# A decoder on one core: two stages rewritten, the maxima and score pieces of the last cross attention and the film sum and bias of the modulation

## The reference, cut to what matters

```python
scores = jnp.einsum('bthd,bghd->bhtg', Q, K) / np.sqrt(DH)
scores = jnp.where(vision_mask[:, None, None, :], scores, -jnp.inf)
topv, topi = jax.lax.top_k(scores, 32)
probs = jax.nn.softmax(topv, axis=-1)
attn = jnp.zeros_like(scores).at[bi, hi, ti, topi].set(probs)
c_t = jnp.einsum('btg,bgd->btd', attn.mean(axis=1), V) * text_mask[..., None]
x = layernorm(x_text, g_norm_in, b_norm_in)
scale_in, shift_in = jnp.split(c_t @ W_film_in + b_film_in, 2, axis=-1)
x = x * (1.0 + mod_gate * scale_in) + mod_gate * shift_in
```

```python
attn = jnp.einsum('bhnd,bhmd->bhnm', q * scale, k)
attn = jax.nn.softmax(attn, axis=-1)
out = jnp.einsum('bhnm,bhmd->bhnd', attn, v)
return out @ proj_w + proj_b
```

## Time and profile before

| | before |
|---|---|
| median of 3 runs | 4454.17 us (4453.13 to 4456.05) |
| the profiled execution's own time | 4449.1 us |
| its span | 4447.3 us |
| granted TensorE clock, mean | 0.819 of full |
| busy: PE, PEld, DVE, ACT, POOL | 76%, 55%, 64%, 41%, 15% |

### The profile page before, as it was taken

One profiled execution on the slowest core, in us unless ns is written; L12 is line 12 of the kernel. 1 busy time (PEld: TensorE's weight loads), 2 busy tenths in 40 slices (PEclk: granted clock), 3 DMA queues, 4 the chain that ended last, 5 costly groups with the idle time before them and its releaser, 6 DMA issues. The chain is left out here.

```text
span 4447.3 us, 71062 instructions
## 1 busy us (share of the span) xinstructions
PE 3383.5 (76%) x21887; PEld 2428.7 (55%) x21951; DVE 2825.5 (64%) x8344; ACT 1819.8 (41%) x5244; POOL 680.4 (15%) x867
## 2 busy tenths in 40 slices
PE   3668379366665885756888867999969997996887
PEld 3546279122223663544556754666657776554777
DVE  6556633599995874365885443444457776566997
ACT  1356234111113663213775333222235554445886
POOL 0044523000003775201000110000000000000000
PEclk9889589566666665577777777999989998998999
DMA  4030167100004000513000000000000000000000
GB/s 115 1 164 0 36 209 234 50 0 0 0 0 154 1 0 18 150 52 90 0 0 0 1 10 0 10 9 9 0 20 0 0 0 3 1 0 15 1 0 19
DMA packets 111454, 152.52 MB, mean 34 GB/s; under 512 B 21594, under 2 KB 88216, under 8 KB 109718
## 3 DMA queue, kind: packets, MB, share of 16 engines
q1 hardware_dynamic: 99822, 142.12, 10.3%
q0 software_dynamic: 11520, 9.05, 0.7%
HBM read 107.45 MB, written 58.50 MB: 37 GB/s over the span
## 5 line engine op out<-in xcount | busy, mean ns | idle before, releaser
L1260 PE MATMUL l_attn_p_s<-l_attn_outer,l_attn_upper 128*128 128x512 f32 x256 | 204.3, 972 | 113.9 <-DVE l_attn_outer L1203 100.0
L95 POOL TENSOR_TENSOR rstd<-vareps,minus_half 128x32 f32<-128x32 f32 x11 | 59.8, 5438 | 1455.7 <-DVE vareps L86 1322.5
L398 ACT ACTIVATE l_ffn_sg<-l_ffn_p_g 112x512 f32<-112x512 f32 x192 | 114.6, 597 | 391.8 <-PE l_ffn_p_g L378 371.9
L409 DVE TENSOR_TENSOR l_ffn_h<-l_ffn_sg,l_ffn_p_u 112x512 f32<-112x512 f32 x192 | 131.8, 687 | 172.6 <-PE l_ffn_p_u L381 172.0
L381 PE MATMUL l_ffn_p_u<-l_ffn_f_xTall,l_ffn_wu 128*112 x384 | 199.1, 600 | 7.3 <-DVE l_ffn_h L409 7.3
L1418 POOL DMA_INDIRECT slots_in<-l_xattn_x,l_xattn_slot x192 | 190.1, 990 | 81.9 <-issue 50.4
L378 PE MATMUL l_ffn_p_g<-l_ffn_f_xTall,l_ffn_wg 128*112 x384 | 199.0, 600 | 0.9 <-DVE l_ffn_al L2450 0.9
L1260 PEld LDWEIGHTS l_attn_p_s<-l_attn_outer,l_attn_upper 128*128 128x128 f32 x256 | 79.2, 324 | 218.6 <-issue 174.2
L387 PEld LDWEIGHTS l_ffn_p_o<-l_ffn_wd,l_ffn_h 112*128 112x128 f32 x1536 | 176.6, 192 | 15.7 <-issue 15.7
L2614 ACT ACTIVATE l_attn_E<-l_attn_p_s,l_attn_nm 128x128 f32<-128x128 f32 x512 | 180.9, 385 | 2.9 <-DVE l_attn_nm L2572 2.9
L387 PE MATMUL l_ffn_p_o<-l_ffn_wd,l_ffn_h 112*128 112x128 f32 x1536 | 176.7, 275 | 0.0
(11 more groups left out here) (790 smaller groups left out, 9505.8 us busy)
## 6 DMA issues: line engine op xcount, KB each, us to landing
l_experts_w<-in_L_ffn_w SPq DMA_DIRECT2D x72, 512.0 KB
slots_in<-l_xattn_empty SPq DMA_DIRECT2D x8, 2145.0 KB, 24.0
shares_out<-l_xattn_zero SPq DMA_DIRECT2D x24, 512.0 KB, 12.5
l_combine_got<-shares_out SPq DMA_DIRECT2D x16, 768.0 KB, 4.5
l_attn_toep<-kernel_rows SPq DMA_DIRECT2D x1, 8192.0 KB, 31.6
xattn_toep<-ssm_rows SPq DMA_DIRECT2D x1, 8192.0 KB
l_slots_w<-in_L_ffn_w SPq DMA_DIRECT2D x32, 176.0 KB
l_experts_x<-slots_in SPq DMA_DIRECT2D x72, 65.0 KB
```

The source lines that it names most:

```text
L398: act.activation(X.sg[:, k % 2], X.p_g[0:X.FP, k % 2], ACT.Silu).then_inc(s.silu_ready, 1)
L409: dve.tensor_tensor(X.h[:, k // X.FC, k % X.FC], X.sg[:, k % 2], X.p_u[0:X.FP, k % 2], ALU.mult).then_inc(s.h_ready, 1)
L1260: mm = pe.matmul(p_s[:, r, a], upper[:], outer[:, r, a * 512:(a + 1) * 512], start=True, stop=True)
```

## The change

In `l3_xattn` the scores of an item are written in one piece, after the whole of the item before has been read; VectorE takes all maxima by one instruction, and ScalarE exponentiates by one. The turned maxima are copied once (`nmT`), without masks; the masks move into a constant, `pick`, which is made once, and 16 matmuls of 128 columns take the place of the 4 of 512.

In `l2_film` VectorE's search is cut: rounds 0 and 1, then the film sum, then rounds 2 and 3. The bias goes to TensorE as three rows of bfloat16 that add up to the float32 row, with a stationary matrix of three rows of ones; the rows are made once by eight instructions at the phase's start, behind the preparation of `wf` and `bf`.

```diff
@@ l2_film, VectorE
+                dve.tensor_copy(ones3[:], R.ones[0:3, :])
...
-                last.then_inc(s.set_ready, 1)
+                chain(last)
+                for r in range(3):
+                    whole = bf[0:3] if r == 0 else brest[:]
+                    chain(dve.tensor_copy(bpart[:], whole))
+                    if r == 0:
+                        chain(dve.tensor_scalar(bparts[:], bpart[:], R.ident[0:3, 0:1], None, ALU.mult))
+                    else:
+                        last = dve.scalar_tensor_tensor(out=bparts[:], in0=bpart[:], scalar=R.ident[0:3, r:r + 1], in1=bparts[:],
+                                                        op0=ALU.mult, op1=ALU.add)
+                        if r == 2:
+                            last.then_inc(s.set_ready, 1)
+                            break
+                        chain(last)
+                    chain(dve.tensor_tensor(brest[:], whole, bpart[:], ALU.subtract))
+                def searched(u, rounds):
+                    for r in rounds:
+                        src = sc[:, u % 2] if r == 0 else wk[:]
+                        for h in range(H):
+                            last = dve.max(top[:, h, 8 * r:8 * r + 8], src[:, h])
+                        if r == TOP // 8 - 1:
+                            last.then_inc(s.top_ready, 1)
+                            break
+                        chain(last)
+                        if r == 0:
+                            dve.tensor_scalar(nm[:], top[:, :, 0], -1.0, None, ALU.mult).then_inc(s.max_ready, 1)
+                        for h in range(H):
+                            last = dve.match_replace(wk[:, h], top[:, h, 8 * r:8 * r + 8], src[:, h], -3e38)
+                        chain(last)
...
-                        for r in range(TOP // 8):
...
+                        searched(u, (0, 1))
                     for b, u in item(3):
                         dve.wait_ge(s.film_done, b + 1)
                         chain(dve.tensor_tensor(f[:], xr[:, u % 2], p_f[:, 0:P], ALU.mult))
                         dve.tensor_tensor(row(xin, b), f[:], p_f[:, P:256], ALU.add).then_inc(s.xin_done, 1)
+                    for b, u in item(1):
+                        searched(u, (2, 3))
@@ l2_film, TensorE
-                    pe.matmul(out[:, 0:256], R.ones[0:1, :], bf[0:1, cols], start=True, stop=False)
+                    pe.matmul(out[:, 0:256], ones3[:], bparts[:, cols], start=True, stop=False)
@@ l3_xattn, VectorE
+                dve.tensor_copy(pick[:], slot4[:].unsqueeze(2).broadcast_to((P, SUB, SC)))
...
-                        for r in range(2):
-                            dve.wait_ge(s.scores_psum, b * 2 + (r + 1))
-                            last = dve.tensor_reduce(nm[:].rearrange("p (j r) -> p j r", j=4)[:, 2 * r:2 * r + 2, 0:SUB],
-                                                     p_s[:, 2 * r:2 * r + 2, 0:SUB * SC].rearrange("p j (m k) -> p j m k", m=SUB), AX.X, ALU.max, negate=True)
-                        last.then_inc(s.max_ready, 1)
+                        dve.wait_ge(s.scores_psum, b + 1)
+                        dve.tensor_reduce(nm[:].rearrange("p (j r) -> p j r", j=4)[:, :, 0:SUB],
+                                          p_s[:, :, 0:SUB * SC].rearrange("p j (m k) -> p j m k", m=SUB), AX.X, ALU.max, negate=True).then_inc(s.max_ready, 1)
...
-                        dve.tensor_tensor(nmB[:], p_c[:, P:256].unsqueeze(1).broadcast_to((P, SUB, P)),
-                                          slot4[:].unsqueeze(2).broadcast_to((P, SUB, P)), ALU.mult).then_inc(s.shift_spread, 1)
+                        dve.tensor_copy(nmT[:], p_c[:, P:256]).then_inc(s.shift_spread, 1)
@@ l3_xattn, ScalarE
-                        for r in range(2):
-                            act.activation(E[0:SC, 2 * r:2 * r + 2], p_s[0:SC, 2 * r:2 * r + 2], ACT.Exp).then_inc(s.exp_ready, 1)
+                        act.activation(E[0:SC], p_s[0:SC], ACT.Exp).then_inc(s.exp_ready, 1)
@@ l3_xattn, TensorE
+                        after(pe, s.exp_ready, b)
                         for j in range(4):
-                            if j % 2 == 0:
-                                after(pe, s.exp_ready, b * 2 - 1 + j // 2)
                             rows = slice(32 * j, 32 * j + 32)
                             mm = pe.matmul(p_s[:, j, 0:SUB * SC], qT[rows, u % 2], kTm[rows, u % 2].rearrange("p m k -> p (m k)"), start=True, stop=True)
-                            if j % 2:
-                                mm.then_inc(s.scores_psum, 1)
+                        mm.then_inc(s.scores_psum, 1)
...
-                        for j in range(4):
-                            rows = slice(32 * j, 32 * j + 32)
-                            mm = pe.matmul(p_s[0:SC, j], R.ones[rows, 0:SC], nmB[rows].rearrange("p m t -> p (m t)"), start=False, stop=True)
+                        for m in range(SUB):
+                            for j in range(4):
+                                rows = slice(32 * j, 32 * j + 32)
+                                mm = pe.matmul(p_s[0:SC, j, m * P:(m + 1) * P], pick[rows, m], nmT[rows], start=False, stop=(m == SUB - 1))
                         mm.then_inc(s.shifted_psum, 1)
```

More of the change, by code:

```diff
@@ L2059, in l2_film @@
         wq, wkv, wf, bf, gate = sb("wq", [P, P]), sb("wkv", [DC, 256]), sb("wf", [P, 512]), sb("bf", [P, 512]), sb("gate", [P, 1])
+        bparts, bpart, brest, ones3 = sb("bparts", [3, 512], BF16), sb("bpart", [3, 512], BF16), sb("brest", [3, 512]), sb("ones3", [3, P], BF16)
         gam, bet, part = sb("gam", [P, P]), sb("bet", [P, P]), sb("part", [P, P])
@@ L2703, in l3_xattn @@
         qT, kTm, va = sb("qT", [P, 2, P]), sb("kTm", [P, 2, SUB, SC]), sb("va", [P, PER, H, 32])
-        nm, nmB, E, oT = sb("nm", [P, P]), sb("nmB", [P, SUB, P]), sb("E", [P, 4, SUB * P]), sb("oT", [P, SUB, P])
+        pick = sb("pick", [P, SUB, SC])
+        nm, nmT, E, oT = sb("nm", [P, P]), sb("nmT", [P, P]), sb("E", [P, 4, SUB * P]), sb("oT", [P, SUB, P])
         rden, heads, headsT, xb = sb("rden", [P, H]), sb("heads", [P, P]), sb("headsT", [P, P]), sb("xb", [P, 2, P])
@@ L2818, in _ @@
                     for b, u in item(3):
-                        pe.wait_ge(s.exp_ready, b * 2 + 2)
+                        pe.wait_ge(s.exp_ready, b + 1)
                         pe.wait_ge(s.va_ready, b + 1)
```

## The result

The changed kernel takes 4462.52 us (median of 13 runs, 4456.78 to 4472.72) against 4456.05 for the one before (13 runs, 4446.47 to 4464.94): ratio 1.0019, 95% interval 1.0011 to 1.0027. It is slower by 6.5 us, and the forecast of 4465 us is 2.5 away. The interval is clear of 1, but the difference is under the 0.2%, 8.9 us, that the prediction took as its mark for a change: by that mark this is "no change", to which it gave 38 in 100, and not "slower", to which it gave 54. The profiled executions have spans of 4447.3 and 4455.0 us, +7.7.

The account below looks back on a forecast made before the run. TensorE's list was taken to set the cross attention's step, and its wandering clock to mix the modulation's steps. Terms 15.5 + 0.5 - 7.4 - 0.8 + 3.1 = +10.9 us gave 4460.0, plus 5.1 for the median: 4465, range 4450 to 4480.

Parts of the forecast that it names:

- The join: Last cross attention: scores, maxima and exponentials in one piece make the step 8.53 us, +15.5 us; bounds -2 and +22.
- The constant `pick`: Last cross attention: making it once, ahead of the fills that the first item waits for, costs +0.5 us.
- The shift: Last cross attention: 16 matmuls of 128 columns in place of four cost nothing, their loads overlapping.
- VectorE's lighter list: Last cross attention: one copy of the turned maxima replaces 0.69 us of `nmB`, but nothing waits for it: 0.
- The start: Modulation: eight VectorE instructions making the bias rows take 4.75 us, partly covered by a wait of 1.65: +3.1 us.
- The modulation's loop: Modulation: moved film sum brings the mean step from 10.24 to 10.0 us, -7.4 us; bounds -18 and +7.
- The end: Modulation, last item: shorter bias matmuls, with nothing covering them, save two times about 0.4 us, -0.8 us.
- Hidden maxima: Rival, last cross attention: the maxima stay hidden, so it gains 2 us instead; 4448 us; 8 in 100.
- The clock in the cross attention: Rival: the clock falls there, every third step having matmuls at 1.2 GHz, +15 us; 4480 us; 10 in 100.
- The clock in the modulation: Rival: TensorE stays at 2.4 GHz, all steps become 9.66 us, 10.6 us less; 4454 us; 12 in 100.
- Faster: Rival, modulation: film sum costs VectorE nothing, clock stays up, steps 9.15 us or less; 4439 us; 8 in 100.
- The modulation only becomes slow: Rival: all modulation steps are long, at about 10.5 us, 15 us more than the sum; 4480 us; 12 in 100.

Follow-up runs that it names:

- two_pieces: The changed kernel with the last cross attention's scores, maxima and exponentials in two pieces again, new shift kept; median step 8.05 us.
- one_max: The changed kernel with scores and exponentials in two pieces again, new shift kept, but one maximum over all four banks; median step 8.52 us.
- old_shift: The changed kernel with the maxima subtracted as before (four masked copies, 4 matmuls of 512 columns), everything still in one piece; median step 8.55 us.
- film_order_only: The kernel before with only the film sum moved between rounds 1 and 2 of the search, float32 bias kept; ratio 0.9991 to before.
- film_pool: Changed modulation, cross attention of before, bias rows made by GpSimd while the first items run instead of by VectorE; ratio 0.9978 to before.

## Why the prediction was right

- *The join, +15.5.* Measured 15.8 between first and last exponential and 15.5 in the phase. One exponential was forecast at 1.87 and took 1.88, one maximum 2.17 and 2.16, the step 8.53 and 8.57; the scores start 2.02 after the exponential and not 1.92, the rest of the round is 0.06 shorter. `two_pieces` and `one_max`, which differ only in the maxima, show the place: the 0.38 us to spare ahead of L2834. By its own terms the upper bound comes to +21, not +22. The constant `pick`, +0.5, took 0.35, and the first exponential came 0.1 later.
- *The shift, 0, and VectorE's lighter list, 0.* Shown by `old_shift`: 8.55 against 8.57. The estimate of 2.4 us a step for loads that are not hidden did not come true.
- *The start, +3.1.* Measured +3.0. The eight instructions took 4.6 us (forecast 4.75, and the 5.8 at the upper end would be 8 x 0.69 = 5.5):

```profile
2084.29 0.41 DVE L2125 CAST l_film_bpart<-l_film_bf 3x512 bf16<-3x512 f32 x1
...
2088.89 0.13 DVE L2168 COPY l_film_nm<-l_film_sc 128x1 f32<-128x1 f32 x1
```

- *The modulation's loop, -7.4: the mis-sized term.* Measured -13.8, inside the bounds of -18 and +7. The kinds of step were right, 9.61 for the short one (9.66) and 10.1 to 10.5 for the long one (10.07), but 23 of the 31 steps are below 9.8, where I kept the old share of four short to six long and added a little for longer ones. The failed step is that I took 10.0 "because a step that is longer for the same matmuls keeps TensorE less busy": TensorE was less busy, 194 of 246 us instead of 217, and the clock rose all the same, from 0.79 to 0.85. I explained the long step by its waits alone and did not lay it beside the clock, which is what tells the two kinds apart. I had also laid the bias into "the reasoning above" without a price; `film_order_only` shows that the order without it wins 0.2 us.
- *The end, -0.8.* Measured +0.7: the short bias matmuls are there, but the last item's products and context sums ran at 1.2 GHz (granted clock 0.50 from 2408 to 2414.6). Two records of a product took 1.22 us, as in this row of after, where the same two took 0.70 before; and the context sums took 1.22 where they took 0.73:

```profile
2410.42 1.22 PE L2233 MATMUL l_film_p_f<-l_film_wf,l_film_cc 128*128 128x256 f32 x2
```

- The sum of the terms was +10.9; the profiles differ by 7.7 and the medians by 6.5. The terms of the modulation were off by -5.0, and the +2.3 of phases with the same code makes up for half of that. The forecast time also started from the 4454.17 of three runs, where the kernel before came out at 4456.05 beside the changed one. That the median came within 2.5 us is in part luck.
- *The rivals.* Hidden maxima: refuted by the row with the wait of 0.45. The clock in the cross attention: it stayed at 1.00. The clock in the modulation: it rose, but reached 1.00 only with added work. Faster: refuted, the step with the film sum inside the search is 9.61 even at a clock of 1.00, not 9.15. The modulation only becomes slow: refuted, the mean step is 9.80, not 10.5.

What stays open: why order and bias together raise the clock to 0.85, while either alone leaves it at 0.75 and 0.77. The runs show the levels and that they set the steps, not which wait tips them. Open too is the old order with a held clock.

## What to carry to other kernels

Before joining two pieces into one instruction, look at what the first piece started early: fewer instructions on an engine with time to spare win nothing, and here a start 0.88 us later against 0.38 to spare cost 0.5 us a step. Where the granted clock of a loop is a mixture, a shorter wait or shorter matmul is worth what it does to the clock; lay each step beside its own clock, hold the clock at full by throwaway matmuls in the waits, and see what the loop is then bound by. Test the halves of a change singly, and together: here 5.0 and 0.2 made 13.8.

## What the runs showed of the hardware that was not expected

GpSimd's work on three partitions slowed VectorE's on 128. In `film_pool` the four mask instructions took 2.79 us, against 1.11 in the changed kernel, while GpSimd's own ran one after the other. VectorE first, then GpSimd:

```profile
2094.00 0.84 DVE L2148 MAX8 l_film_top<-l_film_wk 128x8 f32<-128x120 f32 x4
2094.88 2.79 DVE L2165 SCALAR_TENSOR_TENSOR l_film_e<-l_film_sc,l_film_top,l_film_e 128x120 f32<-128x120 f32 x4
```

```profile
2094.23 1.14 POOL L2102 TENSOR_TENSOR l_film_bparts<-l_film_bparts,l_film_masked 3x512 bf16<-3x512 bf16 x1
2095.45 1.14 POOL L2107 TENSOR_TENSOR l_film_brest<-l_film_brest,l_film_bpart 3x512 f32<-3x512 f32 x1
```

The maxima beside the same kind of GpSimd work kept their 0.84 us for four. In the single records of the trace, the first three of the four mask instructions each end 0.14 to 0.15 us behind one of GpSimd's. The Trainium skill has this ("SBUF — State Buffer", "SBUF: two separate sides"): an instruction of VectorE with two inputs in SBUF and one of GpSimd hold the same pair of ports in turn, each for its whole length. The mask has two such inputs, the search one, and these rows agree. But one input is not always safe here: VectorE's small `tensor_scalar` of the first maxima, which has one and took 0.17 in the kernel before, took 1.04 when GpSimd's next `tensor_tensor` (2099.09, 1.14 us) had started ahead of it:

```profile
2099.22 1.04 DVE L2154 TENSOR_SCALAR l_film_nm<-l_film_top 128x4 f32<-128x4 f32 x1
```
